# Rotation angles laid out per token, another order of transfers and new instruction lists in a four-layer sequence kernel

## The reference, cut to what matters

```python
# layer 0: rotation by two angles of each sequence
out = stack([x0 * ct + x1 * st, -x0 * st + x1 * ct, x2 * cp + x3 * sp, -x2 * sp + x3 * cp], axis=-1)
# layer 1: timestep embedding, adaptive norm, attention with bias and mask, feed-forward
x = t / NUM_STEPS * RESCALE; e = x[:, None] * freqs[None, :]; emb = concatenate([sin(e), cos(e)])
scale, shift = split(silu(emb) @ W_ada + b_ada, 2)
x = _ln(src) * (1.0 + scale) + shift
probs = softmax(where(src_mask, -inf, q @ k / sqrt(8) + attention_bias))     # 16 heads of 8
x = x + (probs @ v) @ Wo + bo
x = x + _gelu2((_ln(x) * g2 + beta2) @ W1 + b1) @ W2 + b2                     # 512 hidden features
# layer 2: adapter 128 -> 32 -> 32 (weights of the sequence's expert) -> 128, residual, layer norm
# layer 3: norm, causal attention, residual, norm, feed-forward with the exact gelu
return x + g * (x2 - x)                                                       # g: gate of the sequence
```

## Time and profile before

| | |
|---|---|
| median of 3 runs | 118.34 us (118.25 to 120.41) |
| profiled execution | 119.0 us, its span 117.2 us |
| mean granted TensorE clock | 0.979 of 2.4 GHz |
| busy in the span | PE 98.4, DVE 86.4, ACT 80.4, POOL 62.8 us |
| table loads of ScalarE | 12, 1.28 us each |
| moved by the DMA engines | 6.33 MB, 5.92 of them on SyncE's queue |

### The profile page before, as it was taken

How to read it: one execution, slowest core, us unless ns; L and a number is a source line. 1 busy time by engine, 2 the same in 40 slices (tenths; PEclk the granted TensorE clock), 3 DMA queues, 4 the chain that set the end, 5 groups by cost and what they waited for, 6 DMA issues and landing times.

```text
span 117.2 us, 5035 instructions
## 1 busy us (share of the span) xinstructions
PE 98.4 (84%) x2156; PEld 74.1 (63%) x2156; DVE 86.4 (74%) x243; ACT 80.4 (69%) x162; POOL 62.8 (54%) x108
## 2 busy tenths in 40 slices
PE   5989079989599999699999889699577997999960
PEld 2337046877367888558876578467446765889950
DVE  3887579899999890756967969999999995301050
ACT  0850013179776899998784998959958999998200
POOL 7004998983985186224358443162445845799400
PEclk9999985999999999999999999999999999999997
DMA  2679999100000000000000000000000000000104
GB/s 48 185 231 250 353 391 378 44 6 6 0 6 6 6 6 6 0 0 6 0 6 3 0 0 6 0 6 6 6 0 0 6 6 6 3 0 6 45 0 134
DMA packets 3904, 6.33 MB, mean 54 GB/s; under 512 B 762, under 2 KB 2970, under 8 KB 3882
## 3 DMA queue, kind: packets, MB, share of 16 engines
q1 hardware_dynamic: 3736, 5.92, 15.1%
q10 hardware_dynamic: 146, 0.09, 0.3%
HBM read 5.48 MB, written 0.52 MB: 51 GB/s over the span
## 4 chain that ended last, share of the span: by engine, by line
DVE 31%; PE 24%; ACT 16%; issue 8%; DMA 7%; SPq 6%; POOL 3%; DVEq 0%; ACTq 0%; POOLq 0%
DMA rows_sb<-in_rows 7%; PE ps L757 6%; DVE ks L949 5%; PE ps L764 5%; ACT vs L562 5%; DVE stats_all L882 4%; DVE peak L972 3%; DVE pt L992 3%; ACT ks L583 3%; POOL rstd L395 2%; DVE norm L1046 2%; DVE sc L961 2%; ACT norm L537 2%; PE ps L748 2%; PE ps L609 2%
## 5 line engine op out<-in xcount | busy, mean ns | idle before, releaser
L395 POOL TENSOR_TENSOR rstd<-mv,half_pow 128x2 f32<-128x2 f32 x20 | 14.5, 725 | 26.7 <-DVE mv L885 26.7
L757 PE MATMUL ps<-feat,w_sb 128*128 128x256 f32 x64 | 16.8, 388 | 0.0
L764 PE MATMUL ps<-w_sb,ks 128*128 128x128 f32 x128 | 16.2, 279 | 0.3 <-ACT ks L583 0.3
L764 PEld LDWEIGHTS ps<-w_sb,ks 128*128 128x128 f32 x128 | 15.4, 191 | 1.2 <-ACT ks L583 0.7
L583 ACT ACTIVATE ks<-ps,cols_sb 128x256 f32<-128x256 f32 x32 | 12.8, 490 | 0.5 <-PE ps L757 0.5
L757 PEld LDWEIGHTS ps<-feat,w_sb 128*128 128x128 f32 x64 | 11.0, 190 | 1.4 <-issue 0.2
L562 ACT COPY vs<-ps 32x256 f32<-32x256 f32 x32 | 11.5, 359 | 0.6
L992 DVE STREAM_TRANSPOSE pt<-sc 128x1024 f32<-128x1024 f32 x8 | 9.8, 1228 | 0.5 <-ACT sc L569 0.5
L949 DVE SCALAR_TENSOR_TENSOR ks<-ps,cols_sb,const_sb 128x1024 f32<-128x1024 f32 x8 | 10.1, 1266 | 0.0
L1021 DVE SCALAR_TENSOR_TENSOR post<-ps,rot,mid_b 128x128 f32<-128x128 f32 x8 | 2.3, 345 | 10.4 <-PE ps L764 10.4
L569 ACT ACTIVATE sc<-sc 128x1024 f32<-128x1024 f32 x8 | 8.3, 1054 | 1.8 <-DVE sc L987 1.1
(11 more groups left out here) (128 smaller groups left out, 237.7 us busy)
## 6 DMA issues: line engine op xcount, KB each, us to landing
bias<-in_fside SPq DMA_DIRECT2D x4, 512.0 KB, 9.2
w_sb<-in_w SPq DMA_DIRECT2D x1, 832.0 KB, 10.9
w_sb<-in_w SPq DMA_DIRECT2D x1, 640.0 KB, 7.1
xin<-in_x SPq DMA_DIRECT2D x4, 128.0 KB, 2.7
out<-post SPq DMA_DIRECT2D x4, 128.0 KB, 1.9
rows_sb<-in_rows SPq DMA_DIRECT2D x1, 448.0 KB, 8.1
w_sb<-in_w SPq DMA_DIRECT2D x1, 192.0 KB, 3.3
const_sb<-in_consts SPq DMA_DIRECT2D x1, 164.5 KB, 2.8
```

The lines of the kernel that those rows point to most:

```text
L395: pool.tensor_tensor(rstd[c][:, :], mv[c][:, :, 1], half_pow[:, :], ALU.pow).then_inc(scale_made[c], 1)
L757: pe.matmul(slot(c, i), wf1[layer][:, i * P:(i + 1) * P], feat[c][:, :], start=True, stop=True).then_inc(ffn1_made[c], 1)
L764: last = pe.matmul(slot(c, 0)[:, t * D:(t + 1) * D], act[c][:, i, t * P:(t + 1) * P], wf2[layer][:, i, :], start=(i == 0), stop=(i == FC - 1))
```

## The change

**Angles.** The host now lays out six angle columns and the gate for each token, on 128 partitions, in one array `smalls` with the embedding's constants (66 columns). VectorE adds a quarter turn to four of the six columns in one operation and reduces them in five; ScalarE writes the sines straight into `rot`, and the two negated ones with a second operation (scale -1). The product that spread the angles, its PSUM slot and the copy out of it are gone. The embedding reads the integer steps directly and has seven operations instead of nine.

**Transfers.** SyncE's order is another one, each chunk of x has its own semaphore, `up_sb` goes out last, the steps are loaded by ScalarE's queue, and ScalarE issues the two loads for the experts only behind the embedding's Silu and a table load. `const_sb` has 198 columns instead of 329.

**Waits.** `transposes_in1c`, `small_operands`, `one_hot_domains` and `spread_k` now wait for the constants themselves; `bv_out10` no longer waits for `rot_set`.

**Lists.** All four lists of `ORDER` are new; of the table, only the ends of TensorE's stand below. The zero products run 9 and 2 times.

```diff
-WARM_UP = (10, 4, 2)
+WARM_UP = (9, 2)
...
-        ffn_in_133 ffn_in_233 ffn_out_b30 ffn_out_c30 ffn_out_b31 ffn_in_333 ffn_out_a32 ffn_out_b32
-        ffn_out_a33 ffn_out_b33 ffn_out_c33 ffn_out_c32 ffn_out_c31""",
...
+        ffn_out_a31 ffn_in_233 ffn_out_b31 ffn_in_333 ffn_out_b32 ffn_out_c32 ffn_out_c31 ffn_out_a33
+        ffn_out_b33 ffn_out_c33""",
...
-                      ("freq", 1), ("turns", 1), ("phase", 1), ("to_tokens", P), ("expert_no", 1),
+                      ("expert_no", 1),
...
+ANGLES = 6
+SMALL = {}
+for _name, _width in [("angles", B // TB * ANGLES), ("gate", B // TB), ("quarter", ANGLES), ("freq", 1),
+                      ("cycles", 1), ("turns", 1), ("phase", 1)]:
+    _at = sum(w for _, w in SMALL.values())
...
-            sp.dma_start(scalar_sb[:, :, :], scalars).then_inc(small_in, 16)
+            def load_x(c):
+                sp.dma_start(xin[c][:, :, :], x[:, c * TILES:(c + 1) * TILES, :]).then_inc(x_in[c], 16)
+
+            def load_bias(c):
+                b0, b1 = c * HB, (c + 1) * HB
+                sp.dma_start(bias[:, b0:b1], fside[:, b0:b1]).then_inc(bias_in[c], 16)
+
+            sp.dma_start(small_sb[:, :], smalls).then_inc(small_in, 16)
+            load_x(0)
+            sp.dma_start(wada_sb[:, :], w_ada).then_inc(wada_in, 16)
             sp.dma_start(const_sb[:, :], consts).then_inc(consts_in, 16)
-            sp.dma_start(steps_sb[:, :], steps.partition_broadcast(P)).then_inc(steps_in, 16)
-            sp.dma_start(xin[0][:, :, :], x[:, 0:TILES, :]).then_inc(x_in[0], 16)
-            sp.dma_start(wada_sb[:, :], w_ada).then_inc(wada_in, 16)
             sp.dma_start(rows_sb[:, 0:2, :], rows[0:2, :].partition_broadcast(P)).then_inc(ada_rows_in, 16)
+            load_x(1)
+            sp.dma_start(w_sb[1][:, 0:NQKV], w1[:, 0:NQKV]).then_inc(wqkv_in, 16)
             sp.dma_start(cols_sb[:, :], cols).then_inc(cols_in, 16)
-            sp.dma_start(w_sb[1][:, 0:NQKV], w1[:, 0:NQKV]).then_inc(wqkv_in, 16)
             for g in range(G):
                 sp.dma_start(mask_u8[g * S:(g + 1) * S, :, :], mask).then_inc(mask_in, 16)
-            for c in range(1, CHUNKS):
-                sp.dma_start(xin[c][:, :, :], x[:, c * TILES:(c + 1) * TILES, :]).then_inc(x_in[1], 16)
-            sp.dma_start(bias[:, 0:HB], fside[:, 0:HB]).then_inc(bias_in[0], 16)
+            load_x(2)
+            load_bias(0)
+            load_x(3)
+            load_bias(1)
             sp.dma_start(w_sb[1][:, NQKV:], w1[:, NQKV:]).then_inc(w_in[1], 16)
             sp.dma_start(rows_sb[:, 2:, :], rows[2:, :].partition_broadcast(P)).then_inc(rows_in, 16)
-            for c in range(1, CHUNKS):
-                b0, b1 = c * HB, (c + 1) * HB
-                sp.dma_start(bias[:, b0:b1], fside[:, b0:b1]).then_inc(bias_in[c], 16)
+            load_bias(2)
+            load_bias(3)
             sp.dma_start(w_sb[3][:, :], w3).then_inc(w_in[3], 16)
+            sp.dma_start(up_sb[:, :], up_wT).then_inc(up_in, 16)
...
-                pool.wait_ge(x_in[min(c, 1)], 16 if c == 0 else 16 * (CHUNKS - 1))
-                pool.wait_ge(rot_set, 1)
+                pool.wait_ge(x_in[c], 16)
+                pool.wait_ge(rot_set, 2)
...
+            sca.dma_start(steps_sb[:, :], steps.partition_broadcast(P)).then_inc(steps_in, 16)
+            sca.preload_act_table_set("silu_and_others")
             sca.dma_start(domain_sb[:, :], domains.partition_broadcast(E + 1)).then_inc(expert_in, 16)
+            sca.wait_ge(angles_set, 1)
+            sca.activation(rot[:, :, 0:ANGLES], angle[:, :, :], ACT.Sin).then_inc(rot_set, 1)
+            sca.activation(rot[:, :, ANGLES:], angle[:, :, ANGLES - 2:], ACT.Sin, scale=-1.0).then_inc(rot_set, 1)
+            sca.wait_ge(consts_in, 16)
+            sca.copy(of_token[:, :, :], ident[:, 0:B].unsqueeze(2).to_broadcast([P, B, S])).then_inc(token_map_set, 1)
+            sca.wait_ge(emb_angle, 1)
+            sca.activation(emb_t[:, :], emb_e[:, :], ACT.Sin).then_inc(emb_sin, 1)
+            sca.wait_ge(emb_sin, 1)
+            sca.activation(emb[:, 0:B], emb_t[:, :], ACT.Silu).then_inc(emb_silu, 1)
...
+                    sca.preload_act_table_set("natural_log_exp_and_others")
...
             sca.dma_start(expert_sb[0:E, :], experts).then_inc(expert_in, 16)
...
-            sca.dma_start(up_sb[:, :], up_wT).then_inc(up_in, 16)
-            sca.preload_act_table_set("silu_and_others")
-            sca.wait_ge(consts_in, 16)
-            sca.copy(of_token[:, :, :], ident[:, 0:B].unsqueeze(2).to_broadcast([P, B, S])).then_inc(token_map_set, 1)
-            sca.wait_ge(angles_set, 1)
-            sca.activation(rot4[:, :, 0:8], angle[:, :, :], ACT.Sin).then_inc(sin_set, 1)
-            sca.wait_ge(emb_angle, 1)
-            sca.activation(emb_t[:, :], emb_e[:, :], ACT.Sin).then_inc(sin_set, 1)
-            sca.wait_ge(sin_set, 2)
-            sca.activation(emb[:, 0:B], emb_t[:, :], ACT.Silu).then_inc(emb_silu, 1)
...
-            pe.wait_ge(consts_in, 16)
-            pe.wait_ge(sin_set, 1)
-            pe.matmul(rot_ps, const("to_tokens", TB),
-                      rot4[:, :, :].rearrange("p t c -> p (t c)"), start=True, stop=True).then_inc(rot_spread, 1)
...
-            keep_clock(WARM_UP[1])
             pe.wait_ge(wada_in, 16)
             pe.wait_ge(emb_silu, 1)
             pe.wait_ge(pool_setup, 2)
             pe.matmul(seq_ps, emb[:, :], wada_sb[:, :], start=True, stop=True).then_inc(seq_made, 1)
-            keep_clock(WARM_UP[2])
+            keep_clock(WARM_UP[1])
...
-                if layer == 1:
-                    pe.wait_ge(rot_set, 1)
-                else:
+                if layer == 3:
...
+                    pe.wait_ge(consts_in, 16)
...
-            def reduce_angle(a, t, turns, phase):
-
-                link(dve.tensor_scalar(t, a, 1 / (2 * np.pi), turns, ALU.mult, ALU.add))
-                link(dve.tensor_scalar(t, t, MAGIC, None, ALU.add))
-                link(dve.tensor_scalar(t, t, -MAGIC, None, ALU.add))
-                link(dve.scalar_tensor_tensor(a, t, -TWO_PI_HI, a, ALU.mult, ALU.add))
-                link(dve.scalar_tensor_tensor(a, t, -float(TWO_PI_LO), a, ALU.mult, ALU.add))
-                link(dve.tensor_scalar(a, a, phase, PI_BELOW, ALU.add, ALU.min))
-                return dve.tensor_scalar(a, a, -PI_BELOW, None, ALU.max)
...
+            angles = small("angles").rearrange("p (t a) -> p t a", a=ANGLES)
+            quarter = small("quarter").unsqueeze(1).to_broadcast([P, B // TB, ANGLES])
             dve.wait_ge(small_in, 16)
-            link(dve.tensor_copy(rot4[:, :, 8], scalar_sb[:, 2, :]))
-            for which in range(2):
-                src = scalar_sb[:, which, :]
-                for i in (0, 1):
-                    dve.tensor_scalar(angle[:, :, 2 * which + i], src, float(np.pi / 2), None, ALU.add)
-                dve.tensor_copy(angle[:, :, 4 + 2 * which], src)
-                last = dve.tensor_scalar(angle[:, :, 5 + 2 * which], src, -1.0, None, ALU.mult)
-            link(last)
-            reduce_angle(angle[:, :, :], turn[:, :, :], 0.0, 0.0).then_inc(angles_set, 1)
-
-
-            dve.wait_ge(consts_in, 16)
+            link(dve.tensor_tensor(angle[:, :, :], angles, quarter, ALU.add))
+            link(dve.tensor_scalar(turn[:, :, :], angle[:, :, :], 1 / (2 * np.pi), MAGIC, ALU.mult, ALU.add))
+            link(dve.tensor_scalar(turn[:, :, :], turn[:, :, :], -MAGIC, None, ALU.add))
+            link(dve.scalar_tensor_tensor(angle[:, :, :], turn[:, :, :], -TWO_PI_HI, angle[:, :, :], ALU.mult, ALU.add))
+            link(dve.scalar_tensor_tensor(angle[:, :, :], turn[:, :, :], -float(TWO_PI_LO), angle[:, :, :], ALU.mult,
+                                          ALU.add))
+            dve.tensor_scalar(angle[:, :, :], angle[:, :, :], PI_BELOW, -PI_BELOW, ALU.min, ALU.max).then_inc(angles_set, 1)
+
+
             dve.wait_ge(steps_in, 16)
-            link(dve.tensor_copy(emb_t[:, :], steps_sb[:, :]))
-            link(dve.tensor_scalar(emb_e[:, :], emb_t[:, :], 40.0, const("freq"), ALU.mult, ALU.mult))
-            reduce_angle(emb_e[:, :], emb_t[:, :], const("turns"), const("phase")).then_inc(emb_angle, 1)
-
-
-            dve.wait_ge(rot_spread, 1)
-            dve.tensor_copy(rot[:, :, :].rearrange("p t c -> p (t c)"), rot_ps).then_inc(rot_set, 1)
+            dve.tensor_scalar(emb_e[:, :], steps_sb[:, :], 40.0, small("freq"), ALU.mult, ALU.mult).then_inc(dve_steps, 1)
+            linked[0] += 1
+            link(dve.tensor_scalar(emb_t[:, :], steps_sb[:, :], small("cycles"), small("turns"), ALU.mult, ALU.add))
+            link(dve.tensor_scalar(emb_t[:, :], emb_t[:, :], MAGIC, -MAGIC, ALU.add, ALU.add))
+            link(dve.scalar_tensor_tensor(emb_e[:, :], emb_t[:, :], -TWO_PI_HI, emb_e[:, :], ALU.mult, ALU.add))
+            link(dve.scalar_tensor_tensor(emb_e[:, :], emb_t[:, :], -float(TWO_PI_LO), emb_e[:, :], ALU.mult, ALU.add))
```

(4 more changed lines are left out.)

176 lines of the change are left out of this document (97 added, 79 removed).

## The result

The changed kernel takes 117.95 us (median of 20 runs), the kernel before 119.32 us in the runs beside it (also 20). The ratio of the two is 0.9893, with a 95% interval of 0.9853 to 0.9932: about 1.3 us faster. The forecast was 3.0 us. Single runs of a kernel differ by one to two per cent, some by more: all ratios here leave the long, disturbed runs out, and since the traces of e4, e7, e8 and e11 are of such runs, places are read from them and sizes only roughly. The profiled execution of the changed kernel has a span of 115.9 us against 117.2.

The account below looks back on a forecast made before the run. No engine was full everywhere: early gains must pass VectorE, then ScalarE, in a chain starting with SyncE's transfer issues. 2.1 us before the end plus 0.9 at the end give 3.0: 118.34 - 3.0 = 115.3 us, range 112.6 to 118.4.

Parts of the forecast that it names:

- The end: After the last post: one output issue instead of three, since chunk 33 now ends last; 0.9 us saved.
- Rotation of chunk 1: GpSimd's second half waits behind rstd_in10; about 1.6 us of VectorE idle time stays before stats_in11, against 1.96.
- One-hots: VectorE's 1.26 us of one-hots move behind modulate10; their data lands 11.3 to 12.2, needed at 12.4: no stall, no margin.
- (b): Rival: the experts' transfer lands at 14.0 to 15.5 and stalls VectorE 1.6 to 3.1 us; 116.9 to 118.4; chance 0.10.
- (c): Rival: the experts' transfer lands at 18.2, as slow as the bias pieces; VectorE stalls 5.8 us; 121.1; chance 0.04.
- Tables: ScalarE: fourteen table loads in all against twelve; the two more cost 2.57 us, cancelling 2.1 us of work done earlier.
- rival (e): ScalarE: a table switch costs as much again in draining as its 1.28 us load; 2.6 us more, 117.9; chance 0.01.
- The front: Start: small_sb lands at 3.0, VectorE rotates chunk 0 from 5.9 instead of 8.95; spread_k10 at 14.4 against 17.65.
- from `spread_k10` to the exponentials: Layer 1: from keys at 14.4, chunk 0's exponential near 23 against 26.70, chunk 1's at 29.5 against 29.82.
- the 2.1 us in front of the end: Layer 1: gelu_013 ends at 66.4 against 68.76; of this 2.4 us, 2.1 are taken and carry through layer 3.
- rival (a): Rival: ScalarE's waits don't shrink, idle for 4 us as before; only 0.9 + 0.3 us remain, 117.1; chance 0.20.
- (d): Rival: front clock stays at 2.4 GHz and chunk 0's 3.7 us arrive whole; 113.7, or 112.6 with more idle gone; chance 0.13.

Follow-up runs that it names:

- e4: The kernel before with the four new lists and nothing else (old angles, old transfer order); ratio to the kernel before 0.9941.
- e7: The changed kernel with the reciprocal of chunk 3 in layer 1 taken by VectorE instead of ScalarE; ratio to the kernel before 0.9931.
- e8: The changed kernel with 14 and 5 filling products instead of 9 and 2 around the embedding's product; ratio to the kernel before 0.9848.
- e11: The changed kernel, w3 and bias pieces of chunks 2 and 3 held until chunk 0's exponential, 6 and 1 filling products; ratio to the kernel before 0.9803.
- e1: The kernel before with SyncE sending the outputs in the order 0, 2, 3, 1; ratio to the kernel before 0.9904.
- e15: As e14 (later transfers in the changed kernel), with 14 and 5 filling products; ratio to the kernel before 0.9688, median 115.13 us.
- e16: As e15, but with the lists of the kernel before (front as in e3) and outputs in the order 0, 2, 3, 1; ratio 0.9858, 117.41 us.
- e5: The changed kernel with one SyncE wait added: w3 is issued only after chunk 0's exponential; ratio to the kernel before 0.9794.
- e13: The changed kernel with w3 issued only when the middle of chunk 0 is written; ratio to the kernel before 0.9749, median 115.89 us.
- e17: As e15, with attn_out10 ahead of project_v11 in TensorE's list; ratio to the kernel before 0.9620, median 114.33 us.
- e14: As e13, and bias pieces of chunks 2 and 3 issued only when chunk 0's scores are made; ratio to the kernel before 0.9712, 115.83 us.
- e12: The changed kernel, w3 and bias pieces of chunks 2 and 3 held until chunk 0's exponential, 14 and 5 filling products; ratio to the kernel before 0.9931.
- e3: The changed kernel with the lists of the kernel before, except one-hots and first norms at VectorE's front; ratio to the kernel before 1.0003.
- e6: The changed kernel with recip13 ahead of the first adapter gelu and TensorE's list to match, 12 table loads; ratio to the kernel before 1.0354.

## Why the prediction was wrong

**What held.** *The end*: forecast 0.9 us, found 1.1 (e1), and the sum was right to keep it apart. *Rotation of chunk 1*: VectorE idle for 1.64 us before `stats_in11`, as said. *One-hots*: no stall for the experts' transfer, so rivals (b) and (c) fall; they took 1.6 us, not 1.26. *The lists*: worth about 2 us (e15 against e16); the forecast's 2.1 was for front and lists together. *Tables*: 14 loads against 12; the drain of rival (e) had no part in it, since between the load at 38.43 (1.28 us) and the gelu at 39.72 there is again only 0.01 us.

**The front was mis-sized, by 0.8 us at the rotation and 1.3 us at the keys.** `small_sb` took 3.20 us to land, the bound that I named and did not take, not the mask pieces' 2.3. The rotation started at 6.73, not 5.9. VectorE's first two multiplications of the rotation then took 0.91 us where they took 0.48, with GpSimd rotating at the same time from 6.66 (0.83 us for its two). `modulate10` came at 12.24 (forecast 11.3), and `spread_k10` at 15.70 (14.4): the one-hots took 0.4 us more than in the sum, and VectorE waited 0.18 us for the keys. This last is the clock's: TensorE, idle for 2.71 us while the embedding was made, was granted 1.2 GHz from 8 to 14 us; the eight `ada` products took 3.78 us, 0.47 each where the next four took 0.30. The sum had no term for that. The same wait is 0.65 us in e5 and 1.08 in e13, and there is none in e8, e15 and e17, whose eight products take 1.99 us:

```profile
16.30 1.28 DVE L969 SCALAR_TENSOR_TENSOR ks<-ps,cols_sb,const_sb 128x1024 f32<-128x1024 f32 x1 [1.08 <-PE ps L707]
```

**The step that failed** is the one from `spread_k10` to the exponentials: "under which TensorE chooses the experts and makes the scores", then near 23 and 29.5. It counted each product's time and took TensorE's instructions as given. Found were 25.50 and 31.84. From keys to exponential the forecast has 8.6 us, the changed kernel takes 9.8 with the hole of 1.45 us in it, e5, e13 and e14 take 8.4, e12, e15 and e17 7.9; from there to chunk 1's exponential it has 6.5, and 6.3 is found. So the 2.5 us that chunk 0's exponential comes late are half the front and half the first hole, and chunk 1 inherits them. The second hole lies behind both and holds up `middle10` (33.84, after VectorE had waited 1.47 us for TensorE). That e15 (23.36 and 30.11) and e17 (23.05 and 29.80) land so near to the forecast's 23 and 29.5 is partly luck: a front 1.1 and 0.8 us late, and a walk from there 0.7 us too long.

In the sum the term that failed is the 2.1 us in front of the end: by the ratios, the change brings 1.3 us and the end alone 1.1, which leaves 0.2. Moving transfers and nothing else brings the rest: the forecast's saving of 3.0 us is a ratio of 0.974, e13 has 0.9749 and e14 0.9712. The holes are why rival (a)'s time, 117.1, a ratio of 0.9895, was nearer than mine.

**Rival (a) had the time and the sign right and the cause wrong.** I had ScalarE's idle time from 28 to 60 us fall from 4.15 to under 2; it stayed at 4.18 (32 less 27.82 busy), the sign I had given for (a). Counted from 14 to 66 us, in the kernel before, the changed one and e15:

```profile
14.00:66.00 52.00, 46.79 (x1093) 36.08 (x1094) 42.55 (x107) 37.29 (x75) 32.70 (x49) 0.97 0.14 53
```

```profile
14.00:66.00 52.00, 44.93 (x1088) 34.22 (x1087) 39.31 (x101) 39.89 (x78) 29.65 (x45) 1.00 0.13 49
```

```profile
14.00:66.00 52.00, 46.95 (x1136) 35.59 (x1141) 41.41 (x106) 41.81 (x80) 31.10 (x47) 1.00 0.15 48
```

ScalarE (the fourth of the five) is idle for 14.7, 12.1 and 10.2 us. The change takes 2.6 us of idle time away and spends 2.57 on two tables, so the last gelus of layer 1 stay where they were. e15 takes 4.5 away, 1.9 after the tables, and its gelus start at 66.08, 2.2 us before the kernel before's. The accounting of the forecast was of the right kind, and part of ScalarE's idle time was not other engines' work but TensorE's missing instructions. But its number for 28 to 60 us was wrong even without collisions: ScalarE is idle there for 3.4 us in e13 and e15 and 3.9 in e14, not under 2. Of the 4.5 us of idle time that e15 takes away, 2.4 lie ahead of 28 us, 0.8 from there to 60 and 1.3 behind.

**The clock, (d).** It did not stay at 2.4 GHz. Where it did (e8), the hole took in that trace what it gave the front. e15, with both mended, has a ratio of 0.9688, 3.7 us under the kernel before: more than the forecast's 3.0. (Its 115.13 us are not to be set beside the forecast's 115.3, which counts from 118.34; the kernel before took 118.99 beside e15.) By its own terms the lower end of (d), and with it the range's, is 112.7 and not 112.6.

What stays open: in e3 the front gains nothing with the old lists although its trace has no hole of this kind over 1 us in layer 1; the wait for `rows_sb` is seen there, its price was not measured. e16, with the front's transfers put in order and the old lists, stands at 0.9858 where e1 has 0.9904, and the intervals overlap: what the new front is worth without the new lists is at most about half a microsecond and not shown. Nor was it tried to thin out a burst, so that its block has the time that it needs.

## What to carry to other kernels

A step that starts earlier starts in other company: when a change brings runs of tiny products forward into the time when data is still loading, look at whether the engine's instructions can keep up, and count products (matmul records), not names; a stall marked "issue" at the same count in two kernels is the sign. Send nothing before it is needed while such runs are near, and put the transfers between two blocks; one wait on SyncE was worth a microsecond here, and more data held back to the wrong moment (e12) lost most of what it had gained. And before crediting a large change with a small gain, try its cheapest part alone: here the order in which four outputs were sent brought as much as the whole.

## What the runs showed of the hardware

TensorE's instructions come in 16 KB packets (17 in a run) over the same DMA engines as the data. Where it ran dry in the front, it did so at product 217 or at 468 (469 in e4 and e16), 251 products apart, whatever they computed. Counted from the product one block (125 or 126 products) ahead, a packet started 0.2 to 1.2 us later with little or no data on its way and 1.7 (e6) to 3.8 us later (e11) under load; it took 0.9 to 1.5 us, and TensorE passed the mark 1.2 to 1.5 us after its end. VectorE's reciprocal of 128x256 numbers out of PSUM took 1.75 us, four times the 0.42 us of the multiplication beside it. After TensorE had stood idle for 2.15 us in e6, the stretch from 58 to 66 us had a mean granted clock of 0.67, and sixteen of its products took 1.9 times as long. Two multiplications of 128x128 numbers took VectorE 0.91 us with GpSimd at the same work and 0.48 without.
